# Two transformer layers for 16 sequences: the loop written out, and the order of the steps redrawn

## What is computed

```python
# layer 0, per item
h  = x + attention(rmsnorm(x), rmsnorm(x), sa_w*)        # 16 heads of 16, 256 keys
h  = h + attention(rmsnorm(h), ctx, ca_w*)               # 16 heads of 16, 77 keys
h  = h + (silu(rmsnorm(h) @ w_gate) * (rmsnorm(h) @ w_up)) @ w_down    # inner width 1024
# layer 1, per item
nF, nX = layernorm(h), layernorm(ctx)
a  = softmax(nF @ nX.T / 16) @ nX
c  = gelu(a @ fc1.T + b1) @ fc2.T + b2                   # inner width 4
nC = layernorm(c)
out = nF + gamma2 * (c + gamma1 * softmax(nC @ nC.T / 16) @ nC)
```

## Time and profile before

| | |
|---|---|
| median of 3 runs | 1125.82 us (1123.43 to 1126.26) |
| the profiled execution | 1126.34 us, its span 1124.4 us |
| TensorE busy | 1003.4 us (89% of the span) |
| VectorE busy | 673.0 us (60%) |
| ScalarE busy | 614.3 us (55%) |
| GpSimd busy | 256.0 us (23%) |
| chain of work that ended last | TensorE 77%, VectorE 12%, ScalarE 4%, issue 5% |
| mean granted TensorE clock | 0.947 of full speed |

### The profile page before, as it was taken

One profiled execution on the slowest core, in us unless ns is written; L12 is line 12 of the kernel. 1 busy time (PEld: TensorE's weight loads), 2 busy tenths in 40 slices (PEclk: granted clock), 3 DMA queues, 4 the chain that ended last, 5 costly groups with the idle time before them and its releaser, 6 DMA issues.

```text
span 1124.4 us, 22748 instructions
## 1 busy us (share of the span) xinstructions
PE 1003.4 (89%) x8556; PEld 818.7 (73%) x8556; DVE 673.0 (60%) x1491; ACT 614.3 (55%) x1300; POOL 256.0 (23%) x305
## 2 busy tenths in 40 slices
PE   2477889999999999999999999999999999988764
PEld 1355577878878888878788787878887877876752
DVE  3524364758576675758485766757585858565532
ACT  4243345374757565665747465656657474746332
POOL 3000011113222231322221221313222212233232
PEclk9676789899999999999999999999999999999985
DMA  5221202021211212121102112121211121101000
GB/s 172 94 79 38 79 27 94 13 78 35 67 60 47 83 42 88 40 87 40 57 34 81 43 58 70 41 89 41 89 41 65 36 78 34 59 4 47 13 10 9
DMA packets 68854, 63.55 MB, mean 57 GB/s; under 512 B 17153, under 2 KB 64166, under 8 KB 68777
## 3 DMA queue, kind: packets, MB, share of 16 engines
q1 hardware_dynamic: 68776, 62.50, 17.0%
...
## 4 chain that ended last, share of the span: by engine, by line
PE 77%; DVE 12%; issue 5%; ACT 4%; DMA 1%; SPq 0%; POOL 0%; DVEq 0%; ACTq 0%
PE ring L899 16%; PE mring L899 15%; PE od L992 9%; PE down_ps L1042 8%; PE ring L978 6%; PE ring L958 5%; DVE mx_sa L747 4%; PE mring L1103 3%; PE ring L1004 3%; PE mring L1115 3%; DVE xn_a L720 2%; PE mring L1052 2%; PE mring L1091 2%; PE mring L1069 2%; PE ring L907 1%
## 5 line engine op out<-in xcount | busy, mean ns | idle before, releaser
L614 ACT ACTIVATE probs<-ring 128x1024 f32<-128x1024 f32 (+1 forms) x192 | 192.7, 1022 | 35.9 <-PE ring L978 32.0
L494 POOL TENSOR_TENSOR hidT_lo<-hid,hidT_hi 128x256 fp32r<-128x256 f32 x128 | 93.6, 731 | 377.1 <-ACT hidT_hi L643 377.1
L747 DVE TENSOR_REDUCE mx_sa<-ring 128x4 f32<-128x1024 f32 x128 | 153.7, 1219 | 19.6 <-PE ring L958 19.1
L958 PE MATMUL ring<-pk_sa 63*128 63x256 f32 x512 | 68.1, 349 | 22.7 <-DVE mx_sa L747 14.3
L752 DVE TENSOR_REDUCE mx_ca<-ring 128x4 f32<-128x308 f32 x128 | 55.4, 475 | 47.0 <-PE ring L958 46.6
L789 DVE SCALAR_TENSOR_TENSOR hid<-hid,mring 128x256 f32<-128x256 f32 x128 | 53.0, 414 | 48.6 <-ACT hid L635 48.6
L1042 PE MATMUL down_ps<-down_hi,hidT_hi 128*128 128x256 f32 x256 | 78.0, 305 | 0.0
L635 ACT ACTIVATE hid<-mring 128x256 f32<-128x256 f32 x128 | 48.6, 380 | 49.5 <-PE mring L899 49.5
L958 PEld LDWEIGHTS ring<-pk_sa 63*128 63x128 f32 x512 | 41.8, 202 | 44.6 <-DVE mx_sa L747 15.1
L992 PE MATMUL od<-probs,vz_sa 128*32 128x256 f32 x1024 | 72.8, 404 | 0.2
L1042 PE MATMUL down_ps<-down_lo,hidT_hi 128*128 128x256 f32 x256 | 72.0, 281 | 0.0
...
## 6 DMA issues: line engine op xcount, KB each, us to landing
pk_sa<-qkT SPq DMA_DIRECT2D x96, 256.0 KB, 2.6
qpk_ca<-qkT SPq DMA_DIRECT2D x48, 256.0 KB, 2.6
x_sb<-x SPq DMA_DIRECT2D x16, 256.0 KB, 2.8
x_res<-x SPq DMA_DIRECT2D x16, 256.0 KB, 3.6
out<-o_sb SPq DMA_DIRECT2D x16, 256.0 KB, 2.8
...
```

Source lines behind the costliest of these rows:

```text
L494: nc.gpsimd.tensor_tensor(hidT[1][:, m % HID, :], hid[:, m % 2, :], hidT[0][:, m % HID, :].bitcast(F32), ALU.subtract).then_inc(S["hidlo"] ...
L614: nc.scalar.activation(granule(g, tag)[0:rows_, i0:i0 + 2, :, :].rearrange("p i h t -> p h i t"), ring_tile(("E", tag, k))[0:rows_].rearra ...
L747: nc.vector.tensor_reduce(mx[tag][:, :, :, k].rearrange("p q h -> p h q"), ps[:].rearrange("p h (q t) -> p h q t", t=T), AX_X, ALU.max).th ...
L958: last = mm(ps[:, half, col:col + kw], qpk[tag][r, slot, q * P:(q + 1) * P], kpk[tag][r, slot, :], start=True, stop=True)
```

## The change

`ORDER` now gives each step one number, in units of a pass; a step of item n is run at the key `number + n`, and each engine's list is the sorted list of all steps of all items. For items 0 to 2 and 13 to 15 a small shift by phase (`SHIFT`) is added to the key. `run` writes everything out: the hardware loop is gone. `RINGS` sorts its users by the fraction of their number, and `before` looks up the last user of the tile in the real order. No step's own instructions change.

```diff
     "pool": """
-        hi.1@-1 ms.sa@2 hi.2@-1 lnstat.nx@-1 hi.3@-1 hi.4@-1 lnstat.nc@-2 hi.5@-1 hi.6@-1 hi.7@-1 bF@-2 ms.mlp@0 ms.ca@1 bC@-2 hi.0@0 lnstat.nf@-1
+        ms.sa@-1.132801 ms.ca@0.681328 ms.mlp@1.498904 hi.0@1.783383 hi.1@1.853236 hi.2@1.917524 lnstat.nx@1.984158 hi.3@2.009518 hi.4@2.015066 hi.5@2.092103
+        hi.6@2.155412 hi.7@2.458468 lnstat.nf@2.762274 bF@2.931165 lnstat.nc@3.068097 bC@3.546435
     """,
...
+SHIFT = {
+    "sa-in": (-0.790308, -0.055933, -0.012761, -0.000645, -0.000224, -0.003959),
...
+    "L1b": (-0.005924, 0.002365, -0.002945, -0.009744, 0.004613, 3.244664),
+}
+EDGE = 3
...
+def in_order(steps):
+
+    return [(step, n) for _, _, step, n in sorted((at + n + shift_of(step, n), k, step, n) for k, (step, at) in enumerate(steps) for n in range(B))]
...
 def users(engine, wanted):
 
-    return [(step, ahead) for step, ahead in STEPS[engine] if wanted(step)]
+    return sorted(((step, at) for step, at in STEPS[engine] if wanted(step)), key=lambda u: u[1] % 1.0)
...
-        def run(eng, engine, todo):
-
-            def one(it):
-                for (name, *args), ahead in STEPS[engine]:
-                    n = it + ahead
-                    if not isinstance(n, int) or 0 <= n < B:
-                        todo[name](n, *args)
-
-            for it in range(-MAX_AHEAD, FIRST):
-                one(it)
-            with eng.Fori(FIRST, LAST) as it:
-                one(it)
-            for it in range(LAST, B - MIN_AHEAD):
-                one(it)
+        def run(engine, todo):
+
+            for (name, *args), n in in_order(STEPS[engine]):
+                todo[name](n, *args)
```

More of the change, by code:

```diff
@@ L66 @@
+        lnstat.nx@1.854666 gu.4@1.946770 gu.5@1.963874 lncen.nx@2.045276 gu.6@2.088755 gu.7@2.111849 dn@2.298752 lnstat.nf@2.704377 lncen.nf@2.794363
+        sc@2.880344 scn@2.954164 lnstat.nc@3.035529 lncen.nc@3.091038 s2@3.195332 p2T@3.327717 pv2@3.459934 out@3.769741
     """,
     "pe": """
-        gu.7@-2 E.ca.2@-1 nCT@-3 oT.sa@0 pv.ca.0@-1 E.ca.3@-1 s2@-3 cT.ca@0 aT.sa@0 pv.ca.1@-1 v.ca@0 oT.ca@-1 wo.sa@0 aT.ca@-1 dnp.5@-2 S.sa.0@1 dnp.6@-2
-        dnp.7@-2 S.sa.1@1 wo.ca@-1 S.sa.2@1 p2T@-3 nXT@-2 S.sa.3@1 S.sa.4@1 pv2@-3 S.sa.5@1 T.mlp@-1 S.sa.6@1 v.sa@1 gu.0@-1 S.sa.7@1 T.ca@0 gu.1@-1 maxT.sa@1
@@ new lines, with phase_of @@
+EDGE = 3
+def phase_of(step):
+    name, tag = (*step, None)[:2]
+    if name in ("ws", "wl"):
+        return None
+    if tag in ("sa", "ca"):
+        return f"{tag}-" + ("in" if name in ("norm", "ms", "xn", "T", "cT", "qk", "v", "pq", "pk") else
+                            "S" if name in ("S", "maxsplit", "maxT", "mr") else "E")
+    if name in ("ldx", "ldc"):
+        return "sa-in" if name == "ldx" else "ca-in"
+    if name in ("ldr", "h1"):
+        return "sa-E"
+    if tag == "mlp" or name in ("gu", "hi", "dnp", "dn"):
+        return "mlp"
+    return "L1b" if tag == "nc" or name in ("nCT", "s2", "s2e", "p2T", "pv2", "bC", "out", "st") else "L1a"
@@ L77, in steps_of, with shift_of @@
+def shift_of(step, n):
+    k = n if n < EDGE else n - (B - 2 * EDGE) if n >= B - EDGE else None
+    phase = phase_of(step)
+    return 0.0 if k is None or phase is None else SHIFT[phase][k]
 def steps_of(engine):
@@ L111 @@
 }
+RING_ORDER = {name: in_order(used) for name, (_, used) in RINGS.items()}
 class Signal:
@@ L125, in not_first @@
 def not_first(n, back=1):
-    return not isinstance(n, int) or n >= back
+    return n >= back
 def at_first(n):
-    return isinstance(n, int) and n == 0
+    return n == 0
 def build(nc, x, ctx, w, vecs, norm_w, fc1t, fc1b, fc2t, fc2b, out):
@@ L325, in before @@
         def before(ring, step, n):
[L327 to L334 removed]
+            tile = tile_of(ring, step)
+            order = RING_ORDER[ring]
+            earlier = [u for u in order[:order.index((step, n))] if tile_of(ring, u[0]) == tile]
+            return earlier[-1] if earlier else None
         def reuse(eng, ring, step, n):
```

73 lines of the change are left out of this document (40 added, 33 removed).

## The result

The changed kernel takes 1143.66 us (median of 4 runs, 1143.22 to 1144.83), the kernel before 1126.04 beside it. The ratio is 1.0158 with a 95% interval of 1.0136 to 1.0180: slower by 1.6%. The forecast was 1142.3. The profiled execution took 1144.83, its span is 1142.7; before, the span was 1124.4, so 18.3 us are to be accounted for.

The account below looks back on a forecast made before the run. The prediction took a steady pass to be a TensorE list with nearly no holes (59.64 of 61.17 us busy). Its terms, -2.3 + 13.0 + 9.8 - 2.0 - 2.0 = +16.5 us, gave a median of 1142.3, range 1118 to 1156.

Parts of the forecast that it names:

- Loop, -2.3: Five looped steady passes at 61.64 us become written-out ones at 61.17: -2.3 us, the longer program costing nothing.
- `bC` beside `xn.mlp`, +13.0: `bC` on GpSimd stretches `xn.mlp` on VectorE to about 2.7 us, delaying `T.mlp`: +1.0 a pass, 13 passes, +13.0 us.
- `E.ca.0` and `E.ca.1` on one tile, +9.8: TensorE waits 0.75 us before `E.ca.1` for ScalarE's exponential of `E.ca.0`, items 1 to 13: +9.8 us.
- The start, -2.0: Item 0's `v.sa` and `ws.9` run in earlier idle time: -2.0 us, between 0 and -5.3.
- The end, -2.0: Item 15's `bF` now runs before the last `lncen.nc`, not beside it: -2.0 us, between -2.1 and 0.
- Edits at nothing: All other reorderings exchange neighbours under another engine's work: no cost; a missing cover would cost tenths of a microsecond a pass.
- rival D: TensorE's longer idle time in each pass halves its clock, 1.7 us each in 13 passes: 1164 us, chance 0.12.
- B: `xn.mlp` gets the VectorE/GpSimd ports before `bC`, or `bC` is held back: -0.6 us a pass, 1121.5 us, chance 0.14.
- C: Neither `bC` nor the shared tile costs anything, the change being a tidier order: 1111.7 us, chance 0.10.
- B2: `bC` costs as said, but TensorE's wait before `E.ca.1` is hidden: 1132.5 us, chance 0.10.
- E: Nothing moves, because something else sets the pass: 1125.8 us, chance 0.02.

Follow-up runs that it names:

- the written-out kernel: The kernel before with its five looped passes written out in the same order, nothing else: 1125.13 us against 1126.1, ratio 0.9983.
- the kernel before with one exchange: The kernel before, loop and all, with `bC` moved between `ms.mlp` and `ms.ca` in GpSimd's list: 1147.55 us against 1126.1.
- the other pair on one tile: The kernel before with `E.ca.0` and `E.ca.1` sharing a tile of `ring`, order of steps unchanged: 1147.07 us against 1127.24.

## Why the prediction was right, and where it was not

- **Loop, -2.3.** Right; shown by the written-out kernel. The 0.47 was a wait before `E.ca.2`, so the sentence that TensorE did not wait between `E.ca.1` and `E.ca.2` holds for the written-out passes only. It is counted once, in this term.
- **`bC` beside `xn.mlp`, +13.0.** The mechanism and the sum held. `xn.mlp` takes 2.45, not 2.7: `bC` had run for 0.31 us before it, where in the earlier trace rows it had run for 0.07 (not 0.1 to 0.2, as the prediction read it). `T.mlp` waits 1.62 (1.7 said), `S.sa.7` waits 0.25 for `v.sa`'s copy (0.15 said), and the wait before `S.sa.4` grew by 0.13, the part of `nXT` that was thought to lie under `T.mlp`'s wait. Sum 0.55 + 1.62 + 0.25 - 1.52 = +0.90 a pass (+1.0 said), 10.8 for items 2 to 13. For item 14 it is 1.4: 2.42 instead of 0.37 before `T.mlp`, less the 0.63 before `T.ca`. Together 12.2, and 13.0 said. The cause is shown from both sides: taken away (`bC` behind, held, early) and put into the kernel before. The Trainium skill, "SBUF — State Buffer", section "SBUF: two separate sides", says that whichever of the two engines starts first keeps the shared ports for its whole instruction. The traces agree where one is clearly first: `xn.mlp` takes 2.45 with `bC` 0.31 ahead, and in the kernel before, at 55.31, a 128x2 operation of GpSimd takes 2.67 instead of 0.69 beside a 128x2048 operation of VectorE that began at 55.15. No run here has `bC` begin during an `xn.mlp`; in the one where `xn.mlp` goes first, `bC` is made to wait for its end.
- **`E.ca.0` and `E.ca.1` on one tile, +9.8.** 0.77 measured for 0.75, twelve times, and 0.79 for items 13 and 14 together: 10.0 in all. Here too both directions were tried. (The range takes 5 to 14 for this term, where its bounds a pass, 0 and 1.11, give 0 to 14; nothing hung on that.) What the text did not see is that a removed wait is not wholly regained (0.25 of 0.39).
- **The start, -2.0.** Too small: the moves are worth 3.1 to 3.5 us, within the stated bound of 5.3. Of this the pass from item 0 to item 1 gave part back: +2.35, of which 0.77 is the first wait of `E.ca.1`, and the rest goes with a longer stretch at half clock, 203.0 to 213.2 us against 206.3 to 213.1. Over both rows of the table the start is -1.3, or -2.0 without `E.ca.1`. The term's size came out right as the sum of two things that were both off, which is luck.
- **The end, -2.0.** `lncen.nc` 0.74 for 2.68, and -1.8 in the last row of the table: right.
- **Edits at nothing.** Right in time, but not for the reason given: `bF` was judged only by `hi.3`, which stands behind it on GpSimd, and its collision with `xn.sa`, 2.2 us of VectorE in most passes, was not seen. It costs nothing because TensorE comes for `xn.sa` some 8 us later.
- **What no term had.** Item 13 to 14 is +3.1, with TensorE idle for 2.0 more and busy for 1.1 more. Of the idle time 1.4 is `bC` (above), 0.2 `E.ca.1`, and 0.4 other waits. The busy time is the clock: it falls behind the wait of 2.42 before `T.mlp`, where before it stayed at full speed at 1000.30:

```profile
1022.20:1025.60 3.40, 3.40 (x17) 3.40 (x17) 1.47 (x8) 0.39 (x1) 0.69 (x1) 0.50 0.00 0
1069.90:1076.70 6.80, 5.03 (x22) 4.63 (x23) 3.34 (x12) 0.98 (x2) 0.85 (x2) 0.50 0.00 0
```

  The second row is the same step of item 15, with twice the 3.4 us at half clock that stood at 1052.8 before. It shows no cost: from item 14 to 15 TensorE is busy for 0.5 more and idle for 0.6 less (-0.1 in the table). So rival D's price was paid about once and not 13 times, and at 1.1 rather than 1.7. The measured terms add up to -2.3 + 12.2 + 10.0 - 2.0 - 1.8 + 1.1 = +17.2. With 0.6 in the two passes of 63.15 and the 0.4 of other waits it is 18.2, and the spans say 18.3. The forecast of +16.5 had 0.8 too much for `bC` and nothing for the clock, the two long passes and the other waits; that the total came within 1.4 of the median owes something to these errors being of opposite sign.
- **The rivals.** B and C fell with `bC` 0.31 us ahead; B2 with the full 0.77 wait; E with the pass. D was right as a mechanism and came near. In the kernel before with one exchange, waits of 1.76 to 1.92 set the clock to half in five of eleven steady passes. With the other pair on one tile it was three of five waits of 1.56, and none of seven of 1.07. In the changed kernel none of its waits of 1.62 did, nor in the three other runs that keep them, 48 waits in all. The Trainium skill, "TensorE: Matmul & The Clock Gate", section "HAM oscillation — how this bites in real kernels", describes a loop that waits for a long transfer in every iteration and has the fall in every iteration; the traces here show it behind much shorter waits, in some passes and not in others. Neither the wait's length nor the steps around it decide alone, since in one execution the same list with the same 1.76 falls in one pass and not in the next. What does stays open; no run varied the wait alone.

Two things stay open beside that. The same lists start in two ways, 4.9 us apart, in different executions. The traces show what goes with it: among the kernels with the changed start, the first fall to half clock comes at 35.3 to 35.7 us in three, with item 0's sum at 197.2 to 197.5, and at 37.4 to 40.7 in five, with the sum at 191.5 to 195.7. Within one kernel the runs lie up to 6 us apart (1107.09 to 1113.49), and the shorter ones have the higher granted clock. Why an execution falls into the one or the other was not found. And the split of a removed wait between shorter pass and longer busy time was read, not explained.
